# Attention with its twelve heads written out, and GpSimd's join of the output halves in two parts

## The reference

```python
x = x + L0_conv_ref(ln_c(x), qkv_w, qkv_b, proj_w, proj_b, rel_pos_h, rel_pos_w)
t = x.reshape(1, 2304, 384)
t = t + L0_ffn_ref(ln_t(t), Wg, bg, W1, b1, W2, b2)      # top 2 of 8 experts, exact gelu

# attention of one head, S = 2304 queries and keys, hd = 32
attn = (q * hd ** -0.5) @ k.T
bias = rel_h[..., :, None] + rel_w[..., None, :]
out  = softmax(attn + bias) @ v
```

## Time and profile before

| | |
|---|---|
| runs, us | 2438.06, 2439.35, 2435.69 |
| profiled execution, us | 2432.83 |
| its span, us | 2431.1 |
| granted TensorE clock, mean | 0.917 |
| busy share of the span: TensorE, VectorE, ScalarE, GpSimd | 86%, 75%, 68%, 30% |
| attention's blocks of 18 units | from 403.44 (first copy of `o_t`) to 1618.92 us (last one) |

### The profile page before, as it was taken

One profiled execution on the slowest core, in us unless ns is written; L12 is line 12 of the kernel. 1 busy time (PEld: TensorE's weight loads), 2 busy tenths in 40 slices (PEclk: granted clock), 3 DMA queues, 4 the chain that ended last, 5 costly groups with the idle time before them and its releaser, 6 DMA issues. The chain is left out here.

```text
span 2431.1 us, 43933 instructions
## 1 busy us (share of the span) xinstructions
PE 2086.6 (86%) x12356; PEld 1889.8 (78%) x12356; DVE 1823.9 (75%) x3335; ACT 1661.7 (68%) x2909; POOL 733.4 (30%) x451
## 2 busy tenths in 40 slices
PE   6833249997998899799889999967599999999997
PEld 6822128886887788688778888846499999999997
DVE  5655367996998799699869998747677777777775
ACT  3344308885887688688768887851277787777775
POOL 0020023443444344344434444442112122122211
PEclk9955569998999899899989999988699999999999
DMA  6788883553554445455444544322367667767764
GB/s 208 230 161 191 174 159 82 94 103 68 98 109 77 97 81 109 76 98 105 79 96 79 109 86 92 91 67 102 115 199 219 218 216 221 221 211 221 226 209 121
DMA packets 123418, 335.17 MB, mean 138 GB/s; under 512 B 17648, under 2 KB 56008, under 8 KB 117860
## 3 DMA queue, kind: packets, MB, share of 16 engines
q1 hardware_dynamic: 111888, 312.42, 51.4%
q0 software_dynamic: 10400, 19.87, 3.8%
q10 hardware_dynamic: 960, 0.80, 0.1%
HBM read 269.62 MB, written 63.43 MB: 137 GB/s over the span
## 5 line engine op out<-in xcount | busy, mean ns | idle before, releaser
L901 DVE TENSOR_REDUCE mx<-ps_m 128x1 f32<-128x384 f32 x1212 | 642.8, 553 | 167.4 <-PE ps_m L750 153.2
L849 ACT ACTIVATE p_hi<-ps_s 128x768 fp32r<-128x768 f32 x648 | 528.1, 815 | 234.6 <-PE ps_s L764 223.3
L598 POOL TENSOR_TENSOR p_lo<-p_f,p_hi 128x768 fp32r<-128x768 f32 x216 | 419.1, 1940 | 746.8 <-ACT p_f L855 746.8
L855 ACT ACTIVATE p_f<-ps_s 128x768 f32<-128x768 f32 x648 | 525.5, 811 | 8.3 <-DVE p_lo L598 5.5
L598 DVE TENSOR_TENSOR p_lo<-p_f,p_hi 128x768 fp32r<-128x768 f32 x432 | 455.0, 1053 | 38.5 <-ACT p_f L855 37.5
L750 PE MATMUL ps_m<-key_hi,query_hi 128*128 128x384 f32 x1240 | 425.1, 349 | 66.5 <-DMA query_hi<-rel_hi_d 39.3
L1593 ACT CAST w_hi<-w_raw 128x384 fp32r<-128x384 f32 x600 | 290.3, 516 | 134.0 <-PE ps_o L1570 126.3
L761 PE MATMUL ps_s<-query_hi,key_hi 128*128 128x384 f32 x1296 | 342.4, 345 | 37.6 <-issue 25.2
L1711 DVE TENSOR_TENSOR w_lo<-w_raw,w_hi 128x384 fp32r<-128x384 f32 x600 | 316.6, 556 | 74.9 <-ACT w_hi L1593 74.7
L774 PE MATMUL ps_o<-p_hi,val 128*65 128x384 f32 x1296 | 335.3, 340 | 37.5 <-issue 33.5
L764 PE MATMUL ps_s<-query_rest,key_rest 121*128 121x384 f32 x1296 | 335.2, 340 | 0.0
(11 more groups left out here) (209 smaller groups left out, 2888.1 us busy)
## 6 DMA issues: line engine op xcount, KB each, us to landing
w_raw<-w_u SPq DMA_DIRECT2D x200, 576.0 KB, 4.8
query_rest<-rel_lo_d SPq DMA_DIRECT2D x36, 864.0 KB
query_rest<-qk_lo_d SPq DMA_DIRECT2D x36, 576.0 KB
query_rest<-qk_hi_d SPq DMA_DIRECT2D x36, 576.0 KB
rel_lo_d<-out_lo SPq DMA_DIRECT2D x6, 1728.0 KB, 31.0
query_hi<-rel_hi_d SPq DMA_DIRECT2D x12, 864.0 KB, 17.4
v_d<-v_sb SPq DMA_DIRECT2D x6, 1170.0 KB, 7.6
val<-v_d SPq DMA_DIRECT2D x12, 585.0 KB, 6.5
```

Source lines behind the costliest of these rows:

```text
L598: engine.tensor_tensor(p_lo[r][:], p_f[idx % 2], p_hi[r][:].bitcast(F32), ALU.subtract).then_inc(lo_done(0, idx)[0], 1)
L849: act.activation(p_hi[r][:], ps_s[:, bank:bank + 2, 0:TB], ACT.Exp).then_inc(hi_ok, 1)
L855: act.activation(p_f[idx % 2], ps_s[:, bank:bank + 2, 0:TB], ACT.Exp).then_inc(f_ok, 1)
L901: dve.tensor_reduce(mx[s // TILES][:, s // 3 % 6, col:col + 1], ps_m[:, c, 0:TB], AX.X, ALU.max).then_inc(mx_ok, 1)
```

## The change

In attention the loop over heads is replaced on all five engines by twelve heads that are written out, so that all wait values are constants. And GpSimd's join is made in two parts of 384 columns (`c` = 0 and 1). The part that ScalarE copied comes behind GpSimd's `p_lo` of unit 2 of the block after, the part that VectorE copied behind that of unit 5, where the whole join was. Each part waits for the copy of its own columns alone, and counts on `low_moved` and `o_sum`, so SP waits for twice the count. The semaphore `o_go`, on which nobody waited, is dropped.

```diff
-        o_go = sem("o_go")
...
             def store(h, par, b):
                 g = (QBLOCKS * par + b) % 2
-                sp.wait_ge(o_sum, QBLOCKS * h + b + 1)
+                sp.wait_ge(o_sum, 2 * (QBLOCKS * h + b + 1))
...
-            with sp.Fori(0, loop_heads // 2) as i:
-                for par in range(2):
-                    rest(2 * i + par, par)
-            rest(HEADS - 2, 0)
+            for h in range(HEADS - 1):
+                rest(h, h % 2)
...
-            def joined(h, par, b, last_one):
+            def joined(h, par, b, c):
 
                 g = (QBLOCKS * par + b) % 2
 
-                pool.wait_ge(acc_a, QBLOCKS * h + b + 2)
-                pool.wait_ge(acc_d, QBLOCKS * h + b + 2)
-
-                pool.wait_ge(*lo_done(h + (b == QBLOCKS - 1), (TILES * (b + 1) + 2 * POOL_EVERY - 1) % UNITS) if not last_one else lo_done(h, UNITS - 1))
-                pool.sem_inc(o_go, 1)
-                pool.tensor_copy(o_low[g][:], o_t[g][HD:2 * HD, :, :]).then_inc(low_moved, 1)
-                pool.wait_ge(low_moved, QBLOCKS * h + b + 1)
-                pool.tensor_tensor(o_s[g][:], o_t[g][0:HD, :, :], o_low[g][:], ALU.add).then_inc(o_sum, 1)
+                pool.wait_ge(acc_a if c == 0 else acc_d, QBLOCKS * h + b + 2)
+                at = TILES * (b + 1) + (1 + c) * POOL_EVERY - 1
+                if at < UNITS:
+                    pool.wait_ge(*lo_done(h, at))
+                elif h < HEADS - 1:
+                    pool.wait_ge(*lo_done(h + 1, at - UNITS))
+                elif c == 0:
+                    pool.wait_ge(*lo_done(h, UNITS - 1))
+                pool.tensor_copy(o_low[g][:, c, :], o_t[g][HD:2 * HD, c, :]).then_inc(low_moved, 1)
+                pool.wait_ge(low_moved, 2 * (QBLOCKS * h + b) + c + 1)
+                pool.tensor_tensor(o_s[g][:, c, :], o_t[g][0:HD, c, :], o_low[g][:, c, :], ALU.add).then_inc(o_sum, 1)
...
                     for b in range(QBLOCKS):
-                        if idx == TILES * (b + 1) + 2 * POOL_EVERY - 1:
-                            joined(h, par, b, last and b == QBLOCKS - 1)
+                        for c in range(2):
+                            if idx == TILES * (b + 1) + (1 + c) * POOL_EVERY - 1:
+                                joined(h, par, b, c)
...
-            with pool.Fori(0, loop_heads // 2) as h0:
-                for par in range(2):
-                    head(2 * h0 + par, par)
-            head(HEADS - 2, 0)
-            head(HEADS - 1, 1, last=True)
+            for h in range(HEADS):
+                head(h, h % 2, h == HEADS - 1)
```

More of the change, by code:

```diff
@@ L576, in phase_attention @@
         block = ctx.enter_context(nc.Block())
-        loop_heads = OALL_HEADS
         def chunk_at(h, par, k):
@@ L672, in rest @@
                         store(h, par, b)
-                start(h + 1, 1 - par, isinstance(h, int) and h == HEADS - 2)
+                start(h + 1, 1 - par, h == HEADS - 2)
                 store(h, par, 2)
@@ L786, in head @@
                         if idx == 0:
-                            pe.wait_ge(kv_in[up], 48 * ((h + 1) // 2 + 1) if isinstance(h, int) else 48 * (h0 + 1 + par))
+                            pe.wait_ge(kv_in[up], 48 * ((h + 1) // 2 + 1))
                         if idx % TILES == 0:
@@ L798, in head @@
                         if s == 0:
-                            pe.wait_ge(hi_in[tp], 48 * ((h + 1) // 2 + 1) if isinstance(h, int) else 48 * (h0 + 1 + par))
+                            pe.wait_ge(hi_in[tp], 48 * ((h + 1) // 2 + 1))
                         pe.wait_ge(mx_ok, number - 1)
@@ L851, in exps @@
                     act.copy(neg_mt[turn][:], ps_s[0:6, bank, TB:TB + P]).then_inc(negt_ok, 1)
-                if not (isinstance(h, int) and UNITS * h + idx < 2):
+                if UNITS * h + idx >= 2:
                     act.wait_ge(*(lo_done(h, idx - 2) if idx >= 2 else lo_done(h - 1, idx - 2 + UNITS)))
@@ L872, in half @@
             def half(h, par):
-                return (h - par) // 2 if isinstance(h, int) else h0
+                return (h - par) // 2
             act.sem_inc(acc_a, 1)
```

## The result

The changed kernel takes 2330.7 us, the median of four runs (2328.14 to 2332.33), against 2437.84 for the kernel before, measured beside it. The ratio is 0.9558, with a 95% interval of 0.9546 to 0.957. The saving is 107 us, 12 more than forecast, and the time lies in the range. The forecast's own narrower range, 2334 to 2353, missed it; the time is that of rival E.

A forecast was written before the change was run, and what follows sets the result against it. TensorE's matmuls in a row were taken as the bound, except at four jumps and late VectorE maxima. Savings 67.7 + 15.3 + 10.2 + 2.4 - 0.3 = 95.3 us, from 2438.1 to 2343 us; range 2328 to 2372.

The forecast's parts named there:

- rival E: Joins and jumps in attention: no loss left at joins, longer jumps in runs than in profile; about 2330 us, 12%.
- four jumps: Attention's loop jumps back four times, stalling TensorE; written-out heads were to save 67.7 us, bounds 0 and 75.
- joins of heads 0 to 9: GpSimd's joins in the attention loop: two parts were to save 0.51 us each, 15.3 us over 30.
- joins already written out: Three joins in the heads behind the loop, where VectorE or TensorE waited longer: 10.2 us to be saved.
- small loss at the join: TensorE's 0.76 us a block where GpSimd's join delays VectorE's `p_lo`; 0.25 was to remain, bounds 0 and 0.76.
- held pair: GpSimd's addition and next `p_lo` without a gap hold VectorE's `p_lo` 3.45 us, costing 3.42 a block; none expected after the change.
- part 2: Forecast section on GpSimd's join: two shorter parts, about 1.5 us each, end before the next `p_lo` is released.
- moved first part: GpSimd's earlier join part: its wait for ScalarE's copy is empty, 1.9 us of idle time left after it.
- A: Joins gain nothing, VectorE losing as much in four small delays as in one: 2358 us, 14%.
- B: Each part of a join costs TensorE what the whole costs now, 38 us more than forecast: 2381 us, 6%.
- C: VectorE held through two GpSimd instructions at every join, slower than the kernel before: 2473 us, 6%.
- D: TensorE stalls for code in written-out heads too, or jump idle time is late data; only joins gain: 2410 us, 5%.

## Why the prediction was right or wrong

The sum, term by term, against the profile after (and the runs, where they isolate a term):

| term | forecast | measured |
|---|---|---|
| four jumps | 67.7 | 72 between runs with and without the loop, 72.6 in the profile of the one with it |
| joins of heads 0 to 9 | 15.3 | 24 (30 blocks from 32.88 to 32.08) |
| joins already written out | 10.2 | 11 (36.30, 36.24 and 33.33 to 32.19, 32.10 and 30.70) |
| last head | 2.4 | 1.3 (27.75 and 27.73 to 27.11 and 27.05) |
| the very end | -0.3 | -0.3 (3.39 to 3.71 from the last copy to the last sum) |

*Jumps.* Right in mechanism and nearly in size. The runs pay some 4 us more than the one profiled execution of before, from which the 67.7 come; the bound of 75 took it in. "No part of it can be left on another engine" was right for this change, but an understatement of the risk.

*The small loss at the join* is the term that was mis-sized, and with it the forecast. I let 0.25 us a join remain, by the thought that each meeting of the two engines delays VectorE a little. With shorter parts it doesn't: at both places VectorE's `p_lo` keeps its 0.95 us and GpSimd waits. The loss is 0, the lower bound; that is 7.5 us of the 12. A part took 2.2 to 2.4 us from the copy's start to the addition's end, not 1.5, because of this waiting, and still ended 0.8 before the release. Of what separates 32.1 from 18 x 1.758 = 31.6, 0.2 is the one wait for a maximum in each block (33 of them above); the rest isn't isolated.

*The held pair.* Here the conclusion of part 2 held and its account was wrong in part. The point at which the pair is held isn't the release itself: additions in the loop ended 0.15 to 0.18 after it too and weren't held. My "narrowly, by 0.26" should have been compared with the loop's own rows, where the same difference was 0.15: `p_f` at 448.10 ended at 448.91, the addition at 449.06.

```profile
448.10 0.81 ACT L855 ACTIVATE p_f<-ps_s 128x768 f32<-128x768 f32 x1
```

The sentence that writing out the join as it is "would spread this loss from 3 joins to 33" came true in kind: written out, with `o_go`, all 33 were held. The loss was smaller than 3.42 in 21 of 32 blocks, 1.9 us, where the clock didn't fall, and the kernel came to 2432.2. Written-out code and the increment are both needed for it: in the loop, with the increment, nothing is held. Without the increment the written-out joins aren't held (2352.4), so "`o_go` and its increment cost nothing" was wrong: with a whole join in written-out heads they cost 80 us. With the join in two parts in the loop their blocks are the same 32.0 to 32.1 us, since in the full blocks each part ends some 0.8 us before the release. In the last head the parts end 0.56 to 0.61 after it, and no pair is held there only because no instruction of VectorE is waiting at that moment. VectorE's `p_lo` comes while GpSimd's late one runs and takes 1.75 to 1.81, a little over the 1.7 that I had given as the most.

*The moved first part*: right in the full blocks. Its wait was empty (GpSimd's copy starts 0.12 after its own `p_lo`), and nothing behind it came late; 0.87 us of idle time were left, not 1.9.

*The rivals.* A (2358) and B (2381) would have shown as blocks of 32.9 and more; none. C, the slower one, is a real mechanism with a smaller price than I gave it: with all joins held it ends at 2432, level with the kernel before, not at 2473. D is refuted by the absence of issue waits of TensorE's matmuls; E came true, in both of its parts.

## What to carry to other kernels

Before a loop is written out or kept, compare the time of its branch with that of another loop in the trace: here a body of some 2200 matmuls and weight loads paid at every jump, and one of some 750 paid nothing. Look at every engine: with four items VectorE stood at each jump and TensorE's own branch was still cheap. All engines have to be freed, because the stalls cover one another. And where VectorE and GpSimd both work on SBUF operands, give GpSimd's side work in pieces that end before its next piece of main work is released, or put a wait on its own result behind it. The wait is worth 73 us where the pair is held, and was some 4 us slower where it isn't. Look for the pair as one VectorE instruction in the trace that lasts several times its usual time and ends its usual time after the second GpSimd instruction.

## What the runs showed of the hardware

A waiting VectorE instruction isn't served in order of arrival. It was passed over by a GpSimd instruction that followed its predecessor without a gap and had been released 0.25 us or more before that one ended (3.44 us instead of 0.95). It went first where the release came 0.15 to 0.18 before the end (1.67), though the records show no gap there either, and where there was a gap of 0.08 us (1.67). The stretch in which the order changes, 0.07 us wide, was crossed by one increment of a semaphore in written-out code. The Trainium skill, SBUF — State Buffer, "SBUF: two separate sides", describes an exclusive lock that belongs to whichever engine starts first. The addition of 1.64 us, begun 0.18 after VectorE's `p_lo`, agrees with it, and so may the one of 1.82, whose start lies within 0.01 of VectorE's; the 33 held `p_lo` don't.

A taken branch of TensorE takes 0.21 us over some 750 or 1500 matmuls and weight loads, 3.4 us over some 3750 in the experts' phase and 4.2 to 10.6 over some 2200 in attention. Why the longer body had the shorter stall is open; no run here separates the phase from the length. Runtime: NRT & Kernel Launch of the Trainium skill, "Instruction fetch mechanics", gives TensorE room for 2048 instructions and most other engines for 512, and says that a jump out of what is held waits for a fetch. With register instructions counted too, TensorE's cheap bodies have 824 and 1646 instructions on record and its dear ones 2634 and 4112, which agrees. VectorE waited at a body of 358 on record and not at one of 180, so its point lies below the 512, and why is open.

TensorE's clock fell after a pause of 2.3 us in 11 blocks of 32 and stayed in 21, with the same instructions on all engines; what decides between them is open.
